# An adaLN block: first modulation as rows, the gate spread by one-hot products, separate banks for each batch's attention

## The chip, the cores and the metric

One core of a Trainium2 chip runs the kernel. The metric is the device time of one execution in microseconds (us), lower is better. TensorE (PE) multiplies, VectorE (DVE), ScalarE (ACT) and GpSimd (POOL) work element by element, SyncE (SP) issues most of the DMAs. TensorE's clock has two levels here, 1.2 and 2.4 GHz; "granted clock" 0.50 and 1.00 in the profile.

## What is computed

```python
mod = (silu(c) @ wmod).reshape(2, 6, 1, 512)         # c: 2 x 512, wmod: 512 x 3072
sa, ca, ga, sb, cb, gb = (mod[:, i] for i in range(6))
ga, gb = (sign(g) * maximum(abs(g), 0.25) for g in (ga, gb))   # sign(0) = 1
h = layernorm(x) * (1 + ca) + sa                     # x: 2 x 512 x 512
x = x + ga * (h @ masked(weight).T + bias)           # 32 x 32 blocks on where the mask has a one
h = layernorm(x) * (1 + cb) + sb
g = silu(lora(h, w1, a1, b1)) * lora(h, w3, a3, b3)  # 512 -> 1376, rank 16, scaling 2
x = x + gb * lora(g, w2, a2, b2)
```

Everything is float32.

## The kernel before

The feature axis of 512 is cut into four slices `k` of 128, the 512 tokens of a batch into four tiles `t` of 128. A product of two float32 matrices is made of three products in the faster fp32r type: high by high, high by low, low by high, where "high" is the rounded value and "low" what is left of it. So each activation and each weight exists as a high part (`ht_hi`, `wa_hi`; written by ACT) and a low part (`ht_lo`, `wa_lo`; written by DVE or POOL). Products on constants at the very start (`WARM_MATMULS`) run while the first loads are under way.

Each engine has one hand-written queue. The order in it is fixed and engines meet at semaphores only, so a waiting instruction holds all that stand behind it.

*Layernorm and turn.* `moment(n)` (DVE), `root` (POOL) and `norm(n)` (DVE or ACT) bring tile n of `work` to mean 0 and variance 1; n runs over 0-3 and 4-7 (attention, batch 0 and 1), 8-11 and 12-15 (feed-forward). `turn(q)` makes four transposes on TensorE, which bring slice k of all four tiles into a PSUM bank with features on partitions. ACT then applies shift and scale twice: `high(q)` writes `ht_hi`, `whole(q)` the unrounded value into `hbuf`, and `low(q)` subtracts them.

*Modulation.* For the attention, shift and scale are made as columns: `mod_column(k)` multiplies 128x128 pieces of `wmod_a` (a copy of a third of `wmod` in another layout, 512 KB each slice) by the two columns of silu(c); one job stands in front of each slice. For the feed-forward they are made as rows, `mod_rows_f`: silu(c), padded to 32 columns, is the stationary operand and four 32-column quads of the array take 256 output columns each; ACT copies the rows out, and two transposes turn them to columns (`columns_f`). `gate_rows(n)` makes the two gates in the same form; ACT and DVE apply sign and maximum.

*Spreading the gate.* The attention's gate must be on all partitions. Four DMAs in ACT's queue (`load_gates`) copy rows of `gates_a` to all 128 partitions of `gate_row_a`, which lies over the mask's tile.

*Attention.* `mask_sum`, `mask_blocks` (one small product) and `mask_weight` make the masked weight of a slice, ACT and DVE split it. `attend(b, k, m)` is the m-th of the three products of slice k, four 512-column matmuls into the four banks `acc`; `attend_last` is slice 3 by tiles. Both batches use the same four banks, so batch 1's bias products (`attend_bias(1)`) wait until DVE has gated batch 0 (`attn_gate`), which waits for the spread gate.

*Feed-forward.* `merge(r)` adds the LoRA product to the r-th weight tile. The loop `for s in range(B * HT)` (22 steps) runs `up` twice (`up_a`, `up_b`) and `down` of the step before. It begins when `turn(8)` to `turn(11)`, `high(8..11)` and `whole(8..11)` are through; their banks are `up_a`, `up_b` and the two `side` banks, and `turn(8)` also waits for DVE to have read `merge(0)` and `merge(1)` from `up_b` and `up_a`.

SP's loads come in this order: x of batch 0, then for each slice `wmod_a`, mask and weight; the attention gate's part of `wmod`; x of batch 1; LoRA pieces 0 and 1; the feed-forward's part of `wmod`; weight tiles.

## Time and profile before

| | |
|---|---|
| median of 3 runs | 280.2 us (279.95 to 282.31) |
| profiled execution, its span | 284.9 us |
| PE / PEld busy | 258.4 / 207.0 us |
| DVE / ACT / POOL busy | 128.4 / 87.6 / 55.6 us |
| DMA | 24.53 MB, mean 86 GB/s |
| mean granted TensorE clock | 0.921 |

The profile is of one execution. Busy time counts what an engine works on and not its waits; PEld is the loading of stationary operands, which overlaps the matmuls. The chain of waits follows the work that ended last back to its releasers. A matmul of two float32 operands stands as two records. Times in the windows and timelines are from the start of the span, and the length of a group of matmuls has the last one's tail in it.

### The profile page before, as it was taken

To read this page: it belongs to the slowest core of one execution; us is meant where nothing else is said; L and a number is where in the kernel's file an instruction comes from. 1 tells how busy PE (TensorE), PEld (TensorE's weight loads), DVE (VectorE), ACT (ScalarE), POOL (GpSimd) and SP (SyncE) were. 2 spreads that over 40 slices of the span, in tenths; PEclk is the share of its full clock that TensorE was granted. 3 is DMA by queue.
4 is the path that set the end of the run, shared out by engine and by line. 5 is a ranking of instruction groups with operands and counts; after the bars stand their busy time and mean duration, and the time that the engine had idled before them with its cause. 6 is when DMAs were issued, how large, how long until landed. Compare 5 with 4: busy or idle time off the path is not lost.

```text
span 284.9 us, 3318 instructions
## 1 busy us (share of the span) xinstructions
PE 258.4 (91%) x1195; PEld 207.0 (73%) x1195; DVE 128.4 (45%) x218; ACT 87.6 (31%) x144; POOL 55.6 (20%) x69
## 2 busy tenths in 40 slices
PE   5799994398875999999999999999999999999991
PEld 3798862385653888888888887788887888888770
DVE  1833251947599399565456554135101111011135
ACT  2341242452933224545654232111011011101110
POOL 1402131655073133033203100005000000000003
PEclk9555799589995999999999999999999999999997
DMA  6999927601512123421332282005800000000004
GB/s 217 371 408 416 363 16 33 30 6 18 185 37 75 37 74 115 131 89 60 90 78 106 56 82 11 2 0 19 156 10 2 0 0 2 0 0 0 2 0 148
DMA packets 12692, 24.53 MB, mean 86 GB/s; under 512 B 1410, under 2 KB 2818, under 8 KB 12676
## 3 DMA queue, kind: packets, MB, share of 16 engines
q1 hardware_dynamic: 11664, 23.65, 28.5%
q10 hardware_dynamic: 1012, 0.67, 4.4%
q8 instruction: 10, 0.16, 0.2%
q14 instruction: 6, 0.05, 0.0%
HBM read 21.16 MB, written 2.10 MB: 82 GB/s over the span
## 4 chain that ended last, share of the span: by engine, by line
PE 82%; DMA 6%; DVE 5%; issue 3%; ACT 3%; SPq 1%; DVEq 0%; ACTq 0%
PE up_a L1003 21%; PE up_b L1003 21%; PE acc L1016 7%; PE acc L1018 7%; PE acc L1017 7%; PE acc L952 6%; PE up_b L885 4%; DMA mask_sb<-gates_a 4%; PE side L867 2%; DMA wmod_a_sb<-in_wmod_a 2%; DVE parts L697 1%; PE side L984 1%; PE acc L937 1%; ACT hbuf L496 1%; DVE wa L707 1%
## 5 line engine op out<-in xcount | busy, mean ns | idle before, releaser
L817 DVE TENSOR_TENSOR g<-up_b,g 128x512 f32<-128x512 f32 (+1 forms) x22 | 15.2, 690 | 73.5 <-PE up_b L1003 73.5
L1016 PE MATMUL acc<-w_hi,g_hi 128*128 128x512 f32 (+1 forms) x88 | 34.9, 396 | 0.0
L1018 PE MATMUL acc<-w_hi,g_lo 128*128 128x512 f32 (+1 forms) x88 | 34.8, 395 | 0.0
L1017 PE MATMUL acc<-w_lo,g_hi 128*128 128x512 f32 (+1 forms) x88 | 34.8, 395 | 0.0
L721 DVE SCALAR_TENSOR_TENSOR raw<-side,raw 128x512 f32<-128x512 f32 (+2 forms) x31 | 20.1, 676 | 27.1 <-PE side L984 20.5
L593 ACT ACTIVATE g<-up_a 128x512 f32<-128x512 f32 (+1 forms) x22 | 13.1, 598 | 61.7 <-PE up_a L1003 61.7
L598 ACT ACTIVATE g_hi<-g 128x512 fp32r<-128x512 f32 (+1 forms) x22 | 13.9, 632 | 52.9 <-DVE g L817 52.9
L390 POOL TENSOR_TENSOR xt<-work,xt 128x512 f32<-128x512 f32 x5 | 6.8, 1377 | 113.0 <-DVE work L736 113.0
L518 ACT ACTIVATE w_hi<-raw 128x512 fp32r<-128x512 f32 (+2 forms) x33 | 20.3, 626 | 26.0 <-DVE raw L721 26.0
L1003 PE MATMUL up_a<-ht_hi,w_hi 128*128 128x512 f32 (+1 forms) x88 | 25.4, 411 | 0.6 <-ACT w_hi L518 0.6
L1003 PE MATMUL up_a<-ht_hi,w_lo 128*128 128x512 f32 (+1 forms) x88 | 24.9, 406 | 0.0
L1003 PE MATMUL up_b<-ht_hi,w_lo 128*128 128x512 f32 (+1 forms) x88 | 24.2, 396 | 0.0
L1003 PE MATMUL up_a<-ht_lo,w_hi 128*128 128x512 f32 (+1 forms) x88 | 24.2, 396 | 0.0
L1003 PE MATMUL up_b<-ht_hi,w_hi 128*128 128x512 f32 (+1 forms) x88 | 24.1, 395 | 0.0
L1003 PE MATMUL up_b<-ht_lo,w_hi 128*128 128x512 f32 (+1 forms) x88 | 24.0, 395 | 0.0
L727 DVE TENSOR_TENSOR w_lo<-raw,w_hi 128x512 fp32r<-128x512 f32 (+2 forms) x33 | 22.4, 707 | 1.9
L1003 PEld LDWEIGHTS up_a<-ht_hi,w_lo 128*128 128x128 f32 (+1 forms) x88 | 16.9, 192 | 4.5
L1003 PEld LDWEIGHTS up_a<-ht_hi,w_hi 128*128 128x128 f32 (+1 forms) x88 | 16.4, 192 | 4.7 <-issue 1.0
L1003 PEld LDWEIGHTS up_a<-ht_lo,w_hi 128*128 128x128 f32 (+1 forms) x88 | 16.6, 188 | 4.3
L1018 PEld LDWEIGHTS acc<-w_hi,g_lo 128*128 128x128 f32 (+1 forms) x88 | 16.6, 188 | 4.1
L1016 PEld LDWEIGHTS acc<-w_hi,g_hi 128*128 128x128 f32 (+1 forms) x88 | 16.5, 188 | 4.0
L1017 PEld LDWEIGHTS acc<-w_lo,g_hi 128*128 128x128 f32 (+1 forms) x88 | 16.5, 188 | 4.0
(107 smaller groups left out, 363.0 us busy)
## 6 DMA issues: line engine op xcount, KB each, us to landing
raw<-in_ffn SPq DMA_DIRECT2D x33, 256.0 KB, 2.7
xt<-in_x SPq DMA_DIRECT2D x8, 256.0 KB, 7.3
wmod_a_sb<-in_wmod_a SPq DMA_DIRECT2D x4, 512.0 KB, 8.0
wmod_sb<-in_wmod SPq DMA_DIRECT2D x2, 1024.0 KB, 13.4
wmod_sb<-in_wmod SPq DMA_DIRECT2D x1, 2048.0 KB, 13.8
out<-xt SPq DMA_DIRECT2D x8, 256.0 KB, 2.9
mask_sb<-in_mask SPq DMA_DIRECT2D x4, 256.0 KB, 8.6
wa<-in_weight SPq DMA_DIRECT2D x4, 256.0 KB, 8.7
```

The lines of the kernel that those rows point to most:

```text
L518: nc.scalar.activation(dst, src, ACT.Copy).then_inc(w_high_ready, 1)
L593: nc.scalar.activation(g[0:w], up_a[0:w], ACT.Silu).then_inc(silu_ready, 1)
L598: nc.scalar.activation(g_hi[s % 2][0:w], g[0:w], ACT.Copy).then_inc(g_high_ready, 1)
L721: nc.vector.scalar_tensor_tensor(w, merge_bank(r)[0:rows, 0:cols], SCALING, w, ALU.mult, ALU.add).then_inc(merged, 1)
L727: nc.vector.tensor_tensor(low_part, src, f32(high), ALU.subtract).then_inc(w_ready, 1)
L817: nc.vector.tensor_tensor(g[0:w], up_b[0:w], g[0:w], ALU.mult).then_inc(g_ready, 1)
L885: last = nc.tensor.matmul(up_b[:, at:at + B], wmod_a_sb[:, k, i, v], silu_c[:, i, 0, 0:B], start=(i == 0), stop=(i == KT - 1))
L952: nc.tensor.matmul(acc[t][:], h[b][:, k, t * P:(t + 1) * P], w[k][:], start=False, stop=False)
L1003: last = nc.tensor.matmul(dst[0:w], w_part[j][:, k, n], h[b][:, k], start=(m == 0 and k == 0), stop=(m == 2 and k == KT - 1))
L1016: nc.tensor.matmul(acc[t][:], hi, down_hi[j][0:w], start=(j == 0), stop=False)
L1017: nc.tensor.matmul(acc[t][:], hi, down_lo[j][0:w], start=False, stop=False)
L1018: last = nc.tensor.matmul(acc[t][:], lo, down_hi[j][0:w], start=False, stop=(j == HT - 1))
```

## The change

- The attention's shift and scale are made as rows, like the feed-forward's: 16 logical products of 256 columns in two halves (`mod_rows_part(0, ...)`), copied by ACT, two transposes, one pair of DVE copies for all slices (`columns`). `wmod_a` and its layout are gone; a third of `wmod` is loaded in two halves of 1 MB instead.
- The gate is made in four quads of 128 columns and spread by four products with a column of the identity, repeated over 128 columns, as stationary operand (`gate_spread`), and ACT copies the bank out (`gate_copy`). The feed-forward's gate is still spread by DMAs, four of 64 KB a batch instead of two of 128.
- Batch 0's attention accumulates in `up_a`, `up_b` and the `side` banks (`front`), batch 1's in `acc`. `turn(0..3)` go to the four `acc` banks, `turn(4..7)` to three of them, `merge(0)` and `merge(1)` to the `side` banks.
- Fifteen products on constants (`fill`) stand at four places of TensorE's queue near the start.
- `attend_last(0)` has only two products a tile, since the first of the three, `attend(0, 3, 0)`, is issued earlier.
- Loads: the two halves of `wmod` are interleaved with the mask and weight of slice 0; x of batch 1 comes ahead of the gate's rows.
- Norms 4 and 5 move from ACT to DVE, `low(0)` from DVE to POOL, and the queues of all engines are reordered.

```diff
-LOW_DVE = (0, 8, 9, 10, 11)
+LOW_DVE = (8, 9, 10, 11)
...
+FILL_MOD, FILL_TURN, FILL_COLS, FILL_H = 6, 2, 4, 3
...
+
+            wmod_sb = sb("wmod_sb", [P, KT, 6 * D], at=early)
...
+        front = [up_a, up_b, *side]
+
         def turn_bank(q):
 
-            return (up_a, up_b)[q % 2] if 2 * KT <= q < 2 * KT + 2 else side[q % 2]
+            i, k = divmod(q, KT)
+            return (acc[k], (acc[1], acc[2], acc[3], acc[1])[k], (up_b, up_a, *side)[k])[i]
+
+        def attn_bank(b, t):
+            return acc[t] if b else front[t]
+
+        def mask_bank(k):
+            return acc[0] if k else side[0]
+
+        def mod_bank(second):
+            return up_a if second else up_b
 
         def merge_bank(r):
-            return (up_b, up_a)[r] if r < FIRST_MERGES else side[SIDE[("merge", r)] % 2]
+            return side[r] if r < FIRST_MERGES else side[SIDE[("merge", r)] % 2]
...
+        def gate_rows_out(n):
+            return (acc[0][:, P:2 * P], front[1][:, 0:P])[n]
...
 
             load_x(0)
-            for k in range(KT):
-                sp.dma_start(wmod_a_sb[:, k], wmod_a[k]).then_inc(wmod_a_loaded[k], 16)
+            load_mod(SHIFT_A, GATE_A, wmod_a_loaded[0], slice(0, KT // 2))
+            sp.dma_start(mask_sb[:, 0], mask[:, 0]).then_inc(mask_loaded[0], 16)
+            load_mod(SHIFT_A, GATE_A, wmod_a_loaded[1], slice(KT // 2, KT))
+            sp.dma_start(wa[:, 0], weight[:, 0]).then_inc(wa_loaded[0], 16)
+            for k in range(1, KT):
                 load_attention(k)
+            load_x(1)
             load_mod(GATE_A, SHIFT_F, wmod_ga_loaded)
-            load_x(1)
             load_lora(0)
             load_lora(1)
             load_mod(SHIFT_F, GATE_F, wmod_f_loaded)
...
+                for q in range(KT):
+                    row = q * QUAD + b
+                    sp.dma_start(gate_row[:, q * P:(q + 1) * P],
+                                 gates_f[row:row + 1].unsqueeze(1).broadcast_to([1, P, P])
+                                 ).then_inc(gate_row_loaded[b], 16)
...
             root(2, 2)
+            low(0)
             low(1)
             low(2)
             low(3)
             root(T, 2)
             root(T + 2, 2)
+            low(KT)
+            low(KT + 1)
+            low(KT + 2)
+            low(KT + 3)
+            spread(0)
             add_x1(0)
             add_x1(1)
-            spread(0)
-            low(KT)
-            low(KT + 1)
             root(2 * T, 2)
             root(2 * T + 2, 2)
-            low(KT + 2)
-            low(KT + 3)
             spread(1)
             for n in range(T, TILES):
...
-            nc.scalar.activation(silu_c[:, :, 1, 0:1], ct[:, :, 1:2], ACT.Silu).then_inc(silu_c_ready, 1)
+            nc.scalar.activation(silu_c[:], ct[:], ACT.Silu).then_inc(silu_c_ready, 1)
...
+                act.wait_ge(centre_ready, n - T * i - 1 + 2 * i)
...
                     act.wait_ge(attn_out, T * (b + 1))
-                else:
-                    act.wait_ge(col_a_ready, k + 1)
+                act.wait_ge(cols_ready, 1 + second)
...
+            def gate_copy(b):
+
+                act.wait_ge(spread_out, b + 1)
+                act.wait_ge(block_on_ready, KT)
+                nc.scalar.activation(gate_row_a[b], acc[2 + b][:], ACT.Copy).then_inc(gate_row_ready, 1)
...
             norm(3)
+            mod_evacuate(0)
             masked_weight_high(0)
             high(0)
             whole(0)
+            masked_weight_high(1)
             high(1)
-            masked_weight_high(1)
             whole(1)
             masked_weight_high(2)
             high(2)
             whole(2)
             masked_weight_high(3)
-            gate_abs(0)
             high(3)
             whole(3)
-            lora_high(0)
-            lora_high(1)
-            act.wait_ge(gates_ready, 1)
-            load_gates(act, 0, 0)
-            load_gates(act, 0, 1)
-            norm(T)
-            norm(T + 1)
             norm(T + 2)
             norm(T + 3)
             high(4)
             whole(4)
+            gate_size(0)
             high(5)
-            mod_evacuate()
             whole(5)
-            lora_high(2)
             high(6)
             whole(6)
-            gate_abs(1)
+            gate_copy(0)
             high(7)
             whole(7)
+            gate_copy(1)
...
             moment(1)
             moment(2)
             moment(3)
-            mask_sum(0)
             norm(0)
             norm(1)
             centres(2)
+            mask_sum(0)
             mask_weight(0)
-            columns_a(0)
+            columns(0)
+            masked_weight_low(0)
             mask_sum(1)
-            masked_weight_low(0)
-            columns_a(1)
             mask_weight(1)
-            low(0)
             mask_sum(2)
             masked_weight_low(1)
-            columns_a(2)
             mask_weight(2)
             mask_sum(3)
             masked_weight_low(2)
-            columns_a(3)
             mask_weight(3)
-            gates_of(0)
-            masked_weight_low(3)
             moment(4)
             moment(5)
+            masked_weight_low(3)
             moment(6)
-            centres(4)
             moment(7)
-            attn_gate(0)
-            attn_gate(1)
-            centres(6)
-            attn_gate(2)
-            attn_gate(3)
+            norm(T)
+            norm(T + 1)
+            centres(T + 2)
+            gates_of(0)
             lora_part(0)
             lora_part(1)
+            for n in range(T):
+                attn_gate(n)
             add_x1(2)
             add_x1(3)
             moment(2 * T)
             moment(2 * T + 1)
-            columns_f()
+            columns(1)
             moment(2 * T + 2)
             moment(2 * T + 3)
+            gates_of(1)
+            lora_part(2)
             for n in range(2 * T, 3 * T):
                 norm(n)
-            gates_of(1)
-            lora_part(2)
             merge(0)
             merge(1)
             weight_low(0)
...
-                pe.wait_ge(normed_by_act, min(2 + T * i, 2 + T))
-                if i != 1:
-                    pe.wait_ge(normed, 2 + T * (i - 1) if i else 2)
-                if q == 2 * KT:
-
-                    pe.wait_ge(merged, FIRST_MERGES)
-                elif q >= 2 and q != 2 * KT + 1:
-
-                    pe.wait_ge(h_ready, q - 1 if q < 2 * KT else q - 3)
+                pe.wait_ge(normed_by_act, min(2 + 2 * i, 4))
+                pe.wait_ge(normed, (2, 4, 8)[i])
+                if i == 1:
+
+                    pe.wait_ge(h_ready, (2, 3, 4, 5)[k])
+                elif i == 2 and k < 2:
+
+                    pe.wait_ge(attn_gated, T)
+                    pe.wait_ge(cols_ready, 2)
+                    pe.wait_ge(gates_ready, 2)
+                elif i == 2:
+
+                    pe.wait_ge(merged, k - 1)
...
-            def mod_column(k):
-
-                pe.wait_ge(wmod_a_loaded[k], 16)
-                if k:
-                    pe.wait_ge(col_a_ready, k)
-                for v in range(2):
-                    at = (2 * k + v) * B
-                    for i in range(KT):
-                        last = nc.tensor.matmul(up_b[:, at:at + B], wmod_a_sb[:, k, i, v], silu_c[:, i, 0, 0:B],
-                                                start=(i == 0), stop=(i == KT - 1))
...
+            def fill(count):
+                for _ in range(count):
+                    nc.tensor.matmul(side[1][:], ht_lo[1][:, 0, 0:P], ht_lo[1][:, 0], start=True, stop=True)
+
+            def mod_rows_part(second, ks):
+
+                for k in ks:
+                    if second:
+                        pe.wait_ge(wmod_f_loaded, 16)
+                        pe.wait_ge(attn_gated, 1)
+                    else:
+                        pe.wait_ge(wmod_a_loaded[k // 2], 16)
+                    for q in range(4):
+                        at = ((SHIFT_A, SCALE_A), (SHIFT_F, SCALE_F))[second][q // 2] * D + q % 2 * HALF
+                        last = nc.tensor.matmul(mod_bank(second)[q * QUAD:(q + 1) * QUAD, 0:HALF], silu_c[:, k],
+                                                wmod_sb[:, k, at:at + HALF], start=(k == 0), stop=(k == KT - 1))
+                if KT - 1 in ks:
+                    last.then_inc(mod_out, 1)
+
+            def columns(second):
+                pe.wait_ge(mod_rows_ready, 1 + second)
+                for c in range(2):
+                    at = second * HALF + c * P
+                    last = nc.tensor.transpose(up_a[:, at:at + P], mod_rows[:, second, c * P:(c + 1) * P], ident[:])
+                last.then_inc(cols_out, 1)
...
                 for k in range(KT):
                     for q in range(4):
-                        at = ((SHIFT_F, SCALE_F)[q // 2] - GATE_A) * D + q % 2 * HALF
...
+                        at = vector * D + q * P
+                        last = nc.tensor.matmul(gate_rows_out(n)[q * QUAD:(q + 1) * QUAD], silu_c[:, k],
+                                                wmod_sb[:, k, at:at + P], start=(k == 0), stop=(k == KT - 1))
                 last.then_inc(gate_out, 1)
+
+            def gate_spread(b):
+
+                pe.wait_ge(gates_ready, 1)
+                pe.wait_ge(h_ready, 6 + b)
+                for q in range(KT):
+                    row = q * QUAD + b
+                    last = nc.tensor.matmul(acc[2 + b][:, q * P:(q + 1) * P], ident[:, row:row + 1].broadcast_to([P, P]),
+                                            gates_a[:], start=True, stop=True)
+                last.then_inc(spread_out, 1)
...
-                nc.tensor.matmul(up_a[:, blocks], const[:, BLOCK_ONES:BLOCK_ONES + P], mask_part[:, blocks],
+                    pe.wait_ge(h_ready, 1)
+                nc.tensor.matmul(mask_bank(k)[:, blocks], const[:, BLOCK_ONES:BLOCK_ONES + P], mask_part[:, blocks],
                                  start=True, stop=True).then_inc(mask_out, 1)
 
             def attend_bias(b):
+                if b:
+
+                    pe.wait_ge(gate_row_ready, B)
+                    pe.wait_ge(h_ready, 2 * KT)
                 for t in range(T):
-                    if b:
-                        pe.wait_ge(attn_gated, t + 1)
-                    nc.tensor.matmul(acc[t][:], ones[:], bias_parts[:], start=True, stop=False)
+                    nc.tensor.matmul(attn_bank(b, t)[:], ones[:], bias_parts[:], start=True, stop=False)
...
-                    nc.tensor.matmul(acc[t][:], ht_hi[b][:, k, tile], wa_hi[k][:], start=False, stop=False)
-                    nc.tensor.matmul(acc[t][:], ht_hi[b][:, k, tile], wa_lo[k][:], start=False, stop=False)
-                    nc.tensor.matmul(acc[t][:], ht_lo[b][:, k, tile], wa_hi[k][:], start=False, stop=True
+                    if b:
+                        nc.tensor.matmul(attn_bank(b, t)[:], ht_hi[b][:, k, tile], wa_hi[k][:], start=False, stop=False)
+                    nc.tensor.matmul(attn_bank(b, t)[:], ht_hi[b][:, k, tile], wa_lo[k][:], start=False, stop=False)
+                    nc.tensor.matmul(attn_bank(b, t)[:], ht_lo[b][:, k, tile], wa_hi[k][:], start=False, stop=True
                                      ).then_inc(attn_out, 1)
...
-                if r == 0:
-
-                    pe.wait_ge(gates_ready, 1)
-                elif r == 1:
-
-                    pe.wait_ge(gates_ready, 2)
+                if r < FIRST_MERGES:
+
+                    pe.wait_ge(attn_gated, T)
...
-            pe.wait_ge(silu_c_ready, 2)
-            mod_column(0)
+            pe.wait_ge(silu_c_ready, 1)
+            mod_rows_part(0, (0, 1))
+            pe.wait_ge(ident_loaded, 16)
+            fill(FILL_MOD)
+            for q in range(KT):
+                turn(q)
             pe.wait_ge(const_loaded, 16)
             mask_blocks(0)
+            fill(FILL_TURN)
+            mod_rows_part(0, (2, 3))
+            fill(FILL_COLS)
+            columns(0)
+            fill(FILL_H)
             pe.wait_ge(ones_ready, 1)
             pe.wait_ge(bias_ready, 1)
+            pe.wait_ge(cols_ready, 1)
+            pe.wait_ge(block_on_ready, 1)
             attend_bias(0)
-            pe.wait_ge(ident_loaded, 16)
-            turn(0)
-            turn(1)
-            mod_column(1)
+            attend(0, 0, 0)
             mask_blocks(1)
-            attend(0, 0, 0)
             attend(0, 0, 1)
-            mod_column(2)
+            attend(0, 0, 2)
             mask_blocks(2)
-            attend(0, 0, 2)
-            turn(2)
             attend(0, 1, 0)
             attend(0, 1, 1)
-            mod_column(3)
             mask_blocks(3)
             attend(0, 1, 2)
-            turn(3)
-            gate_rows(0)
             for m in range(3):
                 attend(0, 2, m)
-            attend_last(0)
-            mod_rows_f()
             turn(4)
             turn(5)
+            gate_rows(0)
+            attend(0, 3, 0)
+            turn(6)
+            gate_spread(0)
+            turn(7)
+            gate_spread(1)
+            attend_last(0)
             attend_bias(1)
             for m in range(3):
                 attend(1, 0, m)
-            columns_f()
-            turn(6)
-            turn(7)
+            mod_rows_part(1, range(KT))
             for m in range(3):
                 attend(1, 1, m)
+            columns(1)
             gate_rows(1)
-            for m in range(3):
-                attend(1, 2, m)
             pe.wait_ge(parts_ready, 2)
             merge(0)
             merge(1)
+            for m in range(3):
+                attend(1, 2, m)
             turn(8)
             turn(9)
...
-        "c": by_feature(c.T),
-        "wmod_a": wmod[:, 0:GATE_A * D].reshape(KT, P, GATE_A, KT, P).transpose(3, 1, 0, 2, 4),
+        "c": np.pad(by_feature(c.T), ((0, 0), (0, 0), (0, QUAD - B))),
```

## Rows read from the trace of the kernel before

**Rows 1.** The page: span, and TensorE's busy time, share and instructions.

```profile
span 284.9 us, 3318 instructions
...
PE 258.4 (91%) x1195; PEld 207.0 (73%) x1195; DVE 128.4 (45%) x218; ACT 87.6 (31%) x144; POOL 55.6 (20%) x69
```

**Rows 2.** The chain of waits in order of time: start us, us, what.

```profile
2.58 5.92 DMA wmod_a_sb<-in_wmod_a
8.63 3.55 PE up_b L885 x16
...
39.84 10.55 DMA mask_sb<-gates_a
...
54.14 1.97 PE side L867 x8
...
89.42 4.68 PE up_a L1003 x12
```

**Rows 3.** Windows: from:to, length, busy of PE, PEld, DVE, ACT, POOL, PEclk, DMA, GB/s.

```profile
7.70:7.90 0.20, 0.00 (x0) 0.00 (x0) 0.20 (x1) 0.20 (x1) 0.00 (x0) 0.50 0.91 307
31.30:31.50 0.20, 0.20 (x2) 0.10 (x2) 0.00 (x0) 0.20 (x1) 0.00 (x0) 0.50 1.08 420
31.70:31.90 0.20, 0.20 (x2) 0.16 (x2) 0.00 (x0) 0.00 (x0) 0.16 (x1) 1.00 1.18 451
54.14:58.80 4.66, 4.66 (x15) 4.08 (x16) 3.64 (x7) 3.47 (x6) 3.91 (x4) 0.50 0.35 25
69.00:72.50 3.50, 2.18 (x16) 1.87 (x15) 2.64 (x5) 1.42 (x3) 2.78 (x3) 1.00 0.56 155
86.20:86.40 0.20, 0.00 (x0) 0.00 (x0) 0.20 (x1) 0.00 (x0) 0.20 (x1) 0.50 0.00 0
93.20:282.00 188.80, 185.41 (x821) 148.72 (x819) 76.57 (x119) 50.86 (x89) 23.93 (x29) 1.00 0.21 45
```

**Rows 4.** Timeline of PE: start us, us, engine, line, operation, count, idle before.

```profile
14.38 1.94 PE L867 MATMUL side<-ident,work 128*128 128x128 f32 x8
...
35.40 0.60 PE L867 MATMUL side<-ident,work 128*128 128x128 f32 x4
35.93 1.93 PE L921 MATMUL up_b<-wmod_sb,silu_c 128*32 128x256 f32 x32
...
38.84 1.08 PE L952 MATMUL acc<-wa_lo,ht_hi 128*128 128x512 f32 x4
...
77.56 1.10 PE L1003 MATMUL up_a<-ht_hi,w_hi 128*128 128x512 f32 x4
```

**Rows 5.** Timeline of ACT, same columns.

```profile
12.76 1.52 ACT L467 ACTIVATE work<-xt,centre,rstd 128x512 f32<-128x512 f32 x2 [4.55 <-DVE centre L636]
...
35.51 0.63 ACT L534 ACTIVATE wa_hi<-wa 128x512 fp32r<-128x512 f32 x1 [3.91 <-DVE wa L677]
...
72.31 0.78 ACT L487 ACTIVATE ht_hi<-up_a,shift,one_plus 128x512 fp32r<-128x512 f32 x1
```

**Rows 6.** Timeline of DVE.

```profile
39.75 0.69 DVE L618 BATCH_NORM_STATS2 stats<-xt 128x6 f32<-128x512 f32 x1
40.47 0.18 DVE L620 BATCH_NORM_AGGREGATE moments<-stats 128x2 f32<-128x6 f32 x1
...
53.66 1.27 DVE L697 SCALAR_TENSOR_TENSOR parts<-parts,const,lora_raw 128x256 fp32r<-128x256 f32 x2
...
68.16 1.28 DVE L697 SCALAR_TENSOR_TENSOR parts<-parts,const,lora_raw 128x1024 fp32r<-128x1024 f32 x1
```

**Rows 7.** Timeline of POOL.

```profile
39.94 1.28 POOL L367 TENSOR_TENSOR ht_lo<-hbuf,ht_hi 128x512 fp32r<-128x512 f32 x1 [6.91 <-ACT hbuf L496]
...
41.99 0.71 POOL L354 TENSOR_TENSOR rstd<-rstd,exponent 128x2 f32<-128x2 f32 x1
```

**Rows 8.** Issues of x1 on SP's timeline, then their median landing in us.

```profile
9.29 5.70 SPq L295 DMA_DIRECT2D xt<-in_x  x4
...
xt<-in_x SPq DMA_DIRECT2D x4, 256.0 KB, 9.8
```

113 lines of the change are left out of this document (40 added, 73 removed).

## The prediction

> **What bounds the kernel now.** I read the page first. Its span is 284.9 us and the matmul engine is busy for 91% of it [rows 1], but that average hides two parts. In the windows, the stretch from 93.2 to 282 us has TensorE busy for 185.4 of 188.8 us at full clock [rows 3]: the feed-forward loop, which the diff leaves alone and which can only start earlier or later. Everything the change can win or lose lies ahead of it. I then read the chain of waits in order of time [rows 2]. It shows two costs: the front waits for the first 512 KB of `wmod_a` (5.92 us) and then runs 16 two-column products in 3.55 us; and from 39.84 us a DMA that spreads the gate takes 10.55 us, over which TensorE stands still until `turn(4)` at 54.14. The granted clock [rows 3] adds a third. It is 0.50 (1.2 GHz) from 7.7 us, after an idle spell, is still 0.50 at 31.3, full (2.4 GHz) at 31.7, and 0.50 again from 54.14 to 58.8, after the gate's stall. Last I read each engine's timeline for the prices [rows 4 to 7].
>
> **Prices.** Eight transposes, which is two `turn`s, are 1.94 us at 1.2 GHz, and four are 0.60 at 2.4 GHz, both with their tail (a `turn` is about 0.9 and 0.45 back to back) [rows 4]. Four 512-column products are 1.08 with their tail, 0.93 apart when full, 0.23 each, so about 0.45 each at half. `gate_rows`, 16 logical products on 32-column quads of 256 columns, is 1.93 at full; a modulation of the same form costs the same, 0.96 for half of it, and twice that at half clock. ACT: a modulation pass 0.78, a weight copy 0.63, two norms 1.52 [rows 5]. DVE: a moment 0.69 and 0.18, about 0.8 the pair; other 512-column passes (norm, merge, masked weight, gating) I put at 0.6 to 0.7 from that 0.69; two early LoRA parts 1.27, the third 1.28 [rows 6]. POOL: a low part 1.28, a root 0.71 [rows 7] behind a short add, 1.15 the pair by estimate.
>
> **The walk through the front, after the change.** I go through the queues in their new order; times are us from the start of the span.
>
> 1. *First modulation.* The first half of the rows is 1 MB instead of 512 KB. The first piece lands at 2.58 + 5.92 = 8.5; 524 KB more at the 420 GB/s of [rows 3] is 1.3, so 9.85. TensorE has stood idle since its warm-up and is at 0.50. Half the rows: 1.9, to 11.8. Six constant products: 2.7, to 14.5. They cost nothing: `turn` needs ACT's norms, which end at 12.76 + 1.52 = 14.3 [rows 5], as now, since the root and centres ahead of them are unmoved (`mask_sum(0)` only moves behind them).
> 2. *Four turns together.* TensorE has then been busy without a break since 9.85. I take two at half (1.8) and two at full (0.9): 17.2. Mask product 0.2 (an estimate: one product, so not above a 512-column one), two fills 0.5, the second half rows 1.0: 18.8. ACT's copy (0.4) lies under four fills (0.9): 19.7; two transposes 0.25, DVE's two small copies 0.3: 20.3. Three fills and the four bias products run to 21.6, over `high(0)` (to 21.1). The first product starts at 21.6, where it starts at about 20 now: the front alone is 1.6 later.
> 3. *Three slices of batch 0.* Nothing but one mask product (0.2) now stands between the products, where each slice had a column job of 3.5 at half clock. A slice is 2.8 + 0.2, against ACT's 0.63 + 0.78 + 0.78. DVE's chain mask product, compare, masked weight, then ACT's copy and `high`, is queued one slice ahead and costs some 0.1 a slice. The third slice ends at 31.0.
> 4. *New gap.* `turn(4)` is late next. ACT's `whole(3)` ends near 30.2; POOL's `low(3)` stands ahead of the roots in its queue (1.3: 31.5), two roots 2.3, DVE's centres 0.3, ACT's two norms 1.5 and some tenths between engines: 36.05. TensorE waits 5 us. At 86.2 us TensorE stands in a shorter wait and has lost the clock [rows 3], so I charge a restart at half. `turn(4)` is still 18.1 earlier than the 54.14 of now, since the gate's DMA is gone, but `attend(0,3)` now lies behind it.
> 5. *Gate by products.* `turn(4)`, `turn(5)` 1.8, `gate_rows` of 128 columns at half clock 1.9: 39.8. From there ACT sets the pace: size 0.3, six passes of `high` and `whole` 4.7, two copies of the spread gate 1.2 (a 512-column copy, priced as the weight copy): 46.1. `gate_spread` has no row: at least 0.25 for four 128-column products, at most a `turn`'s 0.9 each at half clock; I take 0.5, hidden under ACT either way but for 0.4. TensorE's own work here (`attend(0,3,0)`, two turns, `attend_last`) fits beneath: about 9.5 at worst, the clock returning on the way.
> 6. *Batch 1.* It has its own banks, so its bias products wait for the two gate copies alone: 46.2. The gating of batch 0 starts at about 48, after both LoRA parts, which wait in DVE's queue for ACT's copies behind `gate_copy(1)`; `mod_rows_part(1)` needs one gated tile at about 50 and finds it. TensorE: bias 0.9, slice 2.8, rows 1.9, slice 2.8, columns 0.25: 54.9. Then DVE carries it: columns 0.3, two moments 1.6, gates 0.6 (two 128-column passes, an estimate at half of a 512-column one each), third LoRA part 1.3, four norms 2.4: 61.1. TensorE's gate rows, two merges and a slice (4.3) lie beneath that. The two merges on DVE (1.3), two weight copies on ACT with the first overlapping (0.7): `high(8)` at 63.2.
>
> `high(8)` is at 72.31 now [rows 5] and the first `up` product follows at 77.56 [rows 4]; that stretch keeps its instructions and queues. The second step starts with the row at 89.42 [rows 2], after a DVE queue of LoRA parts and merges whose loads were issued once the third LoRA part was done: that moves from about 69.4 to 58.7, so it shifts too. The sum: 72.3 - 63.2 = 9.1 us less.
>
> Priced at nothing: the removed memset of `silu_c` (POOL idles until the moments), the padded `c` (16 times 4 KB, tiny beside the loads), eight small feed-forward gate DMAs in place of four (SP issues them while the loop runs, and the second batch's are needed at its end; uncovered, some us at the very end), and the swap of `x1` with the attention gate's rows: now `x1` is issued last of the two, from 9.29 to 14.99, and takes 9.8 more [rows 8], so both lie there by 24.8, before the moments of batch 1 want them near 27. The page gives the span as the profiled execution's own time; against its 284.9 the sum is 275.8. The median of the runs shown is 280.2, 4.7 below that span; I subtract the same 9.1: **271.1 us**.
>
> **A rule that speaks against step 2.** In [rows 3] the stretch from 69.0 to 72.5 has 2.18 us of TensorE work, more than half of it `turn`s, and the clock stays full; the stretch to 31.7, in which it came back, was mostly 512-column products with one `turn`. Neither shows whether turns bring it back. The Trainium skill, "TensorE: Matmul & The Clock Gate", Part 4 on PE-mode transpose, says that the full clock doesn't engage for transposes since they don't count as busy in the same way. By it steps 2 and 5 would both restart late, near 280 as worked out under the rivals, where my sum stands at 271.
>
> **Rivals.**
> - *A late clock at the front only.* The fills are too short and the clock returns only among the slices. Two more turns at half 0.9, fills, rows and columns 2.0, bias and part of the first slice 2: 4.9 later, 276.0. For it: TensorE was busy without a break from 8.6 to 31 and stayed at 0.50. Against: the largest part of that was two-column products, and none of those are left.
> - *Late at both places.* Turns and 128-column products do nothing for the clock. In step 5 then `attend_last`, the bias and part of a slice run at half too, 4 to 4.5 more: about 280, no change. For it: nothing in the rows shows the clock returning over turns alone. Against: it stayed full over two of them and a wait [rows 3]. The rule of the Trainium skill quoted above would end here.
> - *Slower: half clock all the way to `turn(8)`.* The 19 us of full-rate work behind step 5 and the slices ahead take twice as long, some 15 and 9 more, of which the gap of step 4 absorbs 5: about 290. It decides from the point where products worth 9 us at full clock run at half. Against: in both places now, 4 to 5 us of 512-column products brought the clock back.
> - *Shorter gap in step 4.* The engines are quicker by 2 to 3 us, or the clock is kept: 268.
>
> **How the numbers follow.** Forecast 0.55; late at the front 0.2; late at both 0.08; half all the way 0.04; shorter gap 0.1; 0.03 for what I don't see. The likeliest case's own range is 269 to 273.5 (the split of the clock in step 2, +-0.9; the spread's bounds, 0.4; tenths between engines in six steps, up to 1.5). With the late front and the shorter gap, 267 to 277 leaves out less than 2 in 10. A measurement of this kernel can tell about 1% from no change, that is below 277.4 or above 283.0: faster 0.87, same 0.08, slower 0.05.
>
> **What would show it.** After the change: first products of the slices near 21.6 with the clock full by then (a granted 0.5 there is the late front); a TensorE gap of 5 us ahead of `turn(4)` near 36, put down to ACT's norm; `attend_bias(1)` near 46 released by ACT's gate copy; `turn(8)` near 61 released by DVE's norm; first `up` near 68.5; and from there the same intervals as before. I am wrong if the loop's own part changes length, or if a wait stands where I name none.

## The result

The kernel after the change takes 278.74 us (median of 20 runs, 277.36 to 280.78), the kernel before 282.27 us in the 20 runs beside it (278.9 to 287.98). The ratio is 0.9946, 95% interval 0.9921 to 0.9971: 1.5 us faster against a forecast of 9.1. The ratio leaves out executions more than 1.5% above the kernel's fastest, which are seven of the 20 runs of before (five of them near 287 us) and none of after. Over all 20 of each the means are 282.6 and 278.9 us, 3.7 apart; experiments 2 and 4 show why before has the long ones and that they belong to what the change removes.

The profile of after, its span and TensorE's busy time:

```profile
span 277.0 us, 3318 instructions
...
PE 250.8 (91%) x1196; PEld 197.7 (71%) x1196; DVE 128.4 (46%) x212; ACT 87.0 (31%) x144; POOL 57.2 (21%) x69
```

The two profiles differ by 284.9 - 277.0 = 7.9 us where the ratio gives 1.5. That is the question of this study. The lines of after that answer to [rows 2] and [rows 4], from TensorE's timeline:

```profile
11.09 1.93 PE L890 MATMUL up_b<-wmod_sb,silu_c 128*32 128x256 f32 x16 [5.02 <-DMA wmod_sb<-in_wmod]
12.95 2.93 PE L878 MATMUL side<-ht_lo 128*128 128x512 f32 x6
15.68 2.68 PE L866 MATMUL acc<-ident,work 128*128 128x128 f32 x16
...
22.94 0.39 PE L960 MATMUL up_a<-wa_hi,ht_hi 128*128 128x512 f32 x1
...
32.35 0.63 PE L960 MATMUL side<-wa_hi,ht_lo 128*128 128x512 f32 x2
37.91 1.97 PE L866 MATMUL acc<-ident,work 128*128 128x128 f32 x8 [4.93 <-ACT work L476]
39.81 1.70 PE L916 MATMUL acc<-wmod_sb,silu_c 128*32 128x128 f32 x32
...
47.80 1.09 PE L945 MATMUL acc<-bias_parts,ones 128*128 128x512 f32 x4
...
62.35 0.63 PE L866 MATMUL up_b<-ident,work 128*128 128x128 f32 x4 [1.09 <-issue]
...
69.25 1.14 PE L1009 MATMUL up_a<-ht_hi,w_hi 128*128 128x512 f32 x4
```

The first slice's products start at 22.94, the third slice ends at 33.0, `turn(4)` comes after a wait of 4.93 us that ACT's norm ends, the bias products of batch 1 stand at 47.80, `turn(8)` at 62.35, the first `up` at 69.25. The walk had 21.6, 31.0, 36.05 after 5 us, 46.2, 61.1 and 68.5. The kernel was later than that by up to 2.0 us and by 0.75 at the walk's end; the loop behind is 277.0 - 69.25 = 207.8 us, and 284.9 - 77.56 = 207.3 before [rows 1, 4]. So the times of the new kernel's model held within 2 us (what ended its fifth step did not, see below). What did not hold is what it was subtracted from.

### The profile page after: what moved, and what is told of

It is laid out like the page before. It is cut to its first block, busy times and chain, and to the rows that moved or that the text cites. A ratio compares the mean times of both kernels' runs of the same rounds, so it can differ in the third digit from the quotient of the medians.

```text
span 277.0 us, 3318 instructions
## 1 busy us (share of the span) xinstructions
PE 250.8 (91%) x1196; PEld 197.7 (71%) x1196; DVE 128.4 (46%) x212; ACT 87.0 (31%) x144; POOL 57.2 (21%) x69
## 4 chain that ended last, share of the span: by engine, by line
PE 79%; DVE 8%; issue 4%; ACT 3%; DMA 3%; POOL 1%; SPq 1%; DVEq 0%; ACTq 0%; POOLq 0%
PE up_a L1009 22%; PE up_b L1009 21%; PE acc L1022 7%; PE acc L1024 7%; PE acc L1023 7%; DMA wmod_sb<-in_wmod 3%; PE acc L960 2%; PE side L878 2%; PE acc L866 2%; DVE parts L697 2%; PE side L990 2%; DVE stats L626 1%; ACT hbuf L502 1%; PE up_b L890 1%; ACT ht_hi L493 1%
## 5 line engine op out<-in xcount | busy, mean ns | idle before, releaser
L721 DVE SCALAR_TENSOR_TENSOR raw<-side,raw 128x512 f32<-128x512 f32 (+2 forms) x33 | 21.4, 677 | 27.4 <-PE side L990 20.8
L1009 PEld LDWEIGHTS up_a<-ht_hi,w_lo 128*128 128x128 f32 (+1 forms) x88 | 16.9, 192 | 4.5
L1022 PEld LDWEIGHTS acc<-w_hi,g_hi 128*128 128x128 f32 (+1 forms) x88 | 16.5, 188 | 4.0
L1023 PEld LDWEIGHTS acc<-w_lo,g_hi 128*128 128x128 f32 (+1 forms) x88 | 16.5, 188 | 3.9
## 6 DMA issues: line engine op xcount, KB each, us to landing
wmod_sb<-in_wmod SPq DMA_DIRECT2D x1, 2048.0 KB, 15.6
```

The lines of the kernel that those rows point to most:

```text
L721: nc.vector.scalar_tensor_tensor(w, merge_bank(r)[0:rows, 0:cols], SCALING, w, ALU.mult, ALU.add).then_inc(merged, 1)
L1009: last = nc.tensor.matmul(dst[0:w], w_part[j][:, k, n], h[b][:, k], start=(m == 0 and k == 0), stop=(m == 2 and k == KT - 1))
L1022: nc.tensor.matmul(acc[t][:], hi, down_hi[j][0:w], start=(j == 0), stop=False)
L1023: nc.tensor.matmul(acc[t][:], hi, down_lo[j][0:w], start=False, stop=False)
```

## Experiments

Each kernel ran beside the kernel before on the same chip.

**1. The kernel before, again** (`before_again`, unchanged).

> The kernel before, unchanged, in new executions. Theory A (the clock): the profiled execution of before, 284.9 us of span, was a long one, because its granted clock came back only at 31.5 us, behind three column jobs at half clock (3.2 us each where the fourth took 1.68). Then a profile with a span near 278 shows a column job of 1.7 us earlier than 31 us and the first up product 4 to 6 us earlier than 77.56, and the runs' mean clocks go with their spans. Theory B (the loads): the long execution had slow DMAs (the gate's 10.55 us or the first load's 5.92 us); then a short one has those shorter and the column jobs unchanged. Theory C: all executions have the front of the first profile and differ in the loop.

Median 287.08 us (282.07 to 287.37, 6 runs), with before's 11 runs beside it at 286.81 (279.63 to 287.5); the profiled execution has a span of 285.6. TensorE's timeline, the four column jobs and the first `up`:

```profile
9.26 3.54 PE L885 MATMUL up_b<-silu_c,wmod_a_sb 128*128 128x2 f32 x16 [3.60 <-DMA wmod_a_sb<-in_wmod_a]
...
16.65 3.41 PE L885 MATMUL up_b<-silu_c,wmod_a_sb 128*128 128x2 f32 x16
...
23.91 3.41 PE L885 MATMUL up_b<-silu_c,wmod_a_sb 128*128 128x2 f32 x16
...
33.11 1.84 PE L885 MATMUL up_b<-silu_c,wmod_a_sb 128*128 128x2 f32 x16
...
78.28 1.12 PE L1003 MATMUL up_a<-ht_hi,w_hi 128*128 128x512 f32 x4
```

It is the first profile once more: two column jobs behind the first at half clock, the fourth at full; the clock is back at 32.4 us. On this chip such executions are the rule. The expected short one was not caught here. That the runs' mean clocks go with their times came out in part: 0.921 or 0.922 in 23 of the 24 runs near 287 us whose clock is on record (0.963 in the other), but 0.950 or 0.968 near 282.8 and 0.958 to 0.974 near 279.7.

**2. The kernel before, a third look** (`before_look2`, unchanged).

> The kernel before once more, to catch an execution other than the long one (spans of 284.9 and 285.6, both with the clock back at 31.5). Times of before come in three groups, near 279.6, 282.8 and 287.2 us. Theory A, sharpened: the groups are three moments at which the clock comes back in the front, so a profile of the middle group has it back near 23 to 28 us with the fourth and third column job at 1.8 us, and one of the short group has it back before 21 us. Rival: the front is the same and the loop or a DMA differs.

One run: 280.15 us, span 278.4. The same lines and, from the windows, the granted clock (the column before the last two):

```profile
9.15 3.31 PE L885 MATMUL up_b<-silu_c,wmod_a_sb 128*128 128x2 f32 x16 [3.08 <-DMA wmod_a_sb<-in_wmod_a]
...
16.50 1.84 PE L885 MATMUL up_b<-silu_c,wmod_a_sb 128*128 128x2 f32 x16
...
20.37 1.84 PE L885 MATMUL up_b<-silu_c,wmod_a_sb 128*128 128x2 f32 x16
...
25.60 1.84 PE L885 MATMUL up_b<-silu_c,wmod_a_sb 128*128 128x2 f32 x16
...
47.34 1.97 PE L867 MATMUL side<-ident,work 128*128 128x128 f32 x8 [7.91 <-ACT work L467]
...
70.00 1.10 PE L1003 MATMUL up_a<-ht_hi,w_hi 128*128 128x512 f32 x4
```

ACT's timeline has the pass `high(8)`:

```profile
64.75 0.78 ACT L487 ACTIVATE ht_hi<-up_a,shift,one_plus 128x512 fp32r<-128x512 f32 x1
```

The windows:

```profile
9.40:16.00 6.60, 6.40 (x26) 5.52 (x27) 5.25 (x14) 2.04 (x3) 3.15 (x5) 0.50 1.02 372
16.50:43.00 26.50, 22.39 (x176) 17.49 (x174) 11.12 (x29) 10.26 (x16) 5.87 (x7) 1.00 0.97 301
```

For comparison, `turn(4)` in the first profile of before:

```profile
54.14 1.97 PE L867 MATMUL side<-ident,work 128*128 128x128 f32 x8 [7.88 <-ACT work L467]
```

Same program, and the first job is at half clock here too (3.31), but the clock is back by 16.5 us instead of 31.7 [rows 3]. The column jobs take 1.84 each and the first `up` starts at 70.00, 7.6 us ahead of the 77.56 of [rows 4]. The gate's stall is as long as in the first profile (TensorE waits 7.91, and 7.88 there). Against this execution the 69.25 of after is 0.75 us earlier, and the whole 1.4 (278.4 - 277.0), close to the ratio's 1.5. The other 0.65 lies in the loop, where the clock falls in the first step of both and is back at 85.5 us in after, at 87.9 here. All 65 runs of before beside these kernels fall into three groups: 18 from 278.9 to 280.8 us, 18 from 282.1 to 283.5, 29 from 286.5 to 288.5, with medians of 279.7, 282.8 and 287.2. Spans of before lie some 1.8 us below times (those of after 1.6), so the first profile (284.9) is of the last group. The ratios of the experiments are taken against the lower two groups together, whose shares differ from set to set (their means are 280.6 to 282.1 us), so small differences are read from medians too.

**3. More products at the very start** (`before_warm`).

```diff
-WARM_MATMULS = 10
+WARM_MATMULS = 20
```

> Before with 20 constant products at the start in place of 10, so that TensorE is busy from 1.4 us to about when the first modulation weights land (8.6 us). Theory A: the clock is full when the column jobs begin in every execution, each is 1.7 us instead of 3.3, the long executions are gone and the median is 276 to 279, no slower than after the change (277 to 279). Theory B or C: the median stays within 0.3% of before, with the same spread of 279 to 288.

284.75 us (282.41 to 288.06), ratio 1.0037 (0.9948 to 1.0125): no gain, and theory A's forecast missed. The median lies between two groups of three runs, near 282.6 and near 287; none is near 279.7. The profile, an execution of the long group, shows the first job at full clock and the second at half:

```profile
9.25 1.92 PE L885 MATMUL up_b<-silu_c,wmod_a_sb 128*128 128x2 f32 x16 [0.96 <-DMA wmod_a_sb<-in_wmod_a]
...
15.04 1.94 PE L867 MATMUL side<-ident,work 128*128 128x128 f32 x8 [1.66 <-issue]
16.77 3.41 PE L885 MATMUL up_b<-silu_c,wmod_a_sb 128*128 128x2 f32 x16
```

```profile
11.00:12.60 1.60, 1.19 (x7) 0.98 (x7) 1.54 (x3) 0.00 (x0) 1.30 (x3) 1.00 0.93 283
12.80:15.00 2.20, 0.57 (x2) 0.00 (x0) 1.67 (x6) 1.58 (x3) 0.31 (x1) 0.50 1.04 411
```

The windows put the loss at 12.7 us, among the four bias products: ahead of the wait of 1.66, and behind waits of 0.96 and 0.32 us and the two-column job. A clock that is full when the work starts is not kept through it; whether the waits or the two-column products cost it, this run does not tell.

**4. Products in those holes too** (`before_fill`: 20 at the start and these).

```diff
             attend_bias(0)
+            for _ in range(8):
+                nc.tensor.matmul(side[1][:], ht_lo[1][:, 0, 0:P], ht_lo[1][:, 0], start=True, stop=True)
             pe.wait_ge(ident_loaded, 16)
```

> Before with 20 products at the start and 8 constant products more between the bias products and turn(0), where TensorE waited 1.66 us with 20 products alone and then lost the clock. Theory A: the clock is kept or comes back before the second column job in most executions, the column jobs take 1.8 us each instead of 3.4, the group near 287 is gone and the median is 276 to 279. Rival: two-column products lower the clock whatever stands around them; then the times stay in the three groups, median above 281.

280.25 us (278.71 to 281.52, 12 runs), ratio 0.9928 (0.9892 to 0.9965), beside 17 runs of before with a median of 286.54. The upper two groups are gone with 18 constant products and nothing else; the median is 1.3 us above the top of what I expected. All four column jobs take 1.84 or 1.85 us, but the clock still dips:

```profile
12.00:16.80 4.80, 4.71 (x35) 4.04 (x33) 2.36 (x7) 3.60 (x5) 0.13 (x1) 1.00 1.02 404
17.00:20.20 3.20, 3.20 (x9) 2.53 (x9) 2.73 (x7) 2.08 (x3) 0.74 (x1) 0.50 1.05 408
```

TensorE is busy for 4.71 of the 4.80 us before the fall, with constant products to 14.0, two turns and the second column job. So a hole is not needed for the clock to fall, and the rival of two-column products is not excluded. Theory A stands for what the groups are: the profiles of this program show the early and the late return, and the middle one was seen in the same front of experiment 5. This kernel, whose DMAs and stalls are those of before, is 0.7 to 1.5 us slower than after by the medians (278.74 and 279.55) and no slower by the ratio (0.9928 against 0.9946): 18 constant products in the old kernel bring most of what the whole change brings.

**5. The gate's spread left out of before** (`before_nogate`).

```diff
-            load_gates(act, 0, 0)
-            load_gates(act, 0, 1)
...
-                nc.vector.tensor_tensor(mid[n % T], acc[t][:], gate_row_a[b], ALU.mult).then_inc(attn_gated, 1)
+                nc.vector.tensor_tensor(mid[n % T], acc[t][:], xt[:, b, t], ALU.mult).then_inc(attn_gated, 1)
```

> Before with the four DMAs that spread the attention's gate left out; the gating multiplies by x instead, which lies there already, so the gate is left out of the result. It prices the stall by itself: 54.14 us for turn(4) should become about 46.5 (ACT's norms right behind their moments, nothing in ACT's queue ahead), so 6 to 8 us less than before, if the stall is what the profile says. If the stall is hidden in ordinary executions, less than 2 us.

272.91 us (270.92 to 280.21, 4 runs), ratio 0.9669 (0.9553 to 0.9785), some 9 us. The four runs look like the three groups again (270.9 and 271.1; 274.7; 280.2); if they are, they lie 8.7, 8.1 and 7.0 us under those of before, so the stall is worth 7 to 9 us, about what I expected. It shrinks to 1.66 us, and the clock is kept through it.

```profile
28.72 1.84 PE L881 MATMUL up_b<-silu_c,wmod_a_sb 128*128 128x2 f32 x16
...
44.20 1.09 PE L863 MATMUL side<-ident,work 128*128 128x128 f32 x8 [1.66 <-ACT work L467]
```

In this execution the clock came back at 23.4 us, between the other two, with the third and fourth job at 1.84: the middle group. So there was a stall worth 7 to 9 us to remove, and the change removed it. It must have put something in its place.

What made the stall is also a matter of order. DVE's timeline in experiment 2:

```profile
43.68 1.29 DVE L707 TENSOR_TENSOR wa<-acc,mask_sb 128x512 f32<-128x512 f32 x2 [6.71 <-DMA mask_sb<-gates_a]
```

The centres for ACT's last two norms stand behind these two gatings in DVE's queue and wait with them for the gate's DMA. Putting them ahead, or issuing the four DMAs from another queue than ACT's, are cheaper changes that were not tried.

**6. The spread left out of after** (`after_nogate2`: no `gate_spread`, no `gate_copy`, gating by x).

> After the change with the spreading of the attention's gate left out (no spread products, no ACT copies, the gating multiplies by x, so the gate is left out of the result). Theory: the spread has been moved from DMA to TensorE and ACT and still costs 2 to 3 us there, two copies of 0.6 in ACT's queue and the waits between spread and turn; so 2 to 3 us less than after the change, against 8 us for the same cut in before. If it is hidden now: under 0.5 us.

276.81 us (276.49 to 277.32), ratio to before 0.9818 (0.9731 to 0.9904), so 1.9 to 2.7 us below after (278.74 and 279.55), about as expected. The spread still costs that much; the rest of the 7 to 9 went elsewhere. With the spread left out of both kernels, these runs lie 5.8 us above the lowest two of before (270.9 and 271.1): without the stall the new order is the slower one.

**7. The spread by DMA again, banks kept** (`after_dmagate`).

```diff
+            for b in range(B):
+                for q in range(KT):
+                    row = q * QUAD + b
+                    act.dma_start(gate_row_a[b][:, q * P:(q + 1) * P],
+                                  gates_a[row:row + 1].unsqueeze(1).broadcast_to([1, P, P])
+                                  ).then_inc(gate_row_a_loaded[b], 16)
```

> After the change with the one part undone: the attention's gate is spread by DMAs again (eight of 64 KB, issued by ACT behind whole(7)) in place of the one-hot products and copies; the banks of their own stay. If the one-hot spread is what takes the stall away: gating of batch 0 starts at 54 to 57 us instead of 49.2, 4 to 7 us slower than after the change. If the separate banks alone take it away: within 1 us of after the change.

290.52 us (289.25 to 291.19), ratio 1.0344 (1.0268 to 1.0419): 11 to 12 us slower than after, more than expected. ACT's and TensorE's timelines:

```profile
44.62 12.21 ACTq L580 DMA_DIRECT2D mask_sb<-gates_a  x8
57.20 1.99 ACT L543 ACTIVATE parts<-lora_raw 128x256 fp32r<-128x256 f32 x3 [11.86 <-issue]
```

```profile
60.03 3.64 PE L897 MATMUL up_a<-wmod_sb,silu_c 128*32 128x256 f32 x32 [10.58 <-DVE wa L714]
```

Eight issues hold ACT's queue for 12.21 us, the LoRA parts wait behind them, the gating behind those, and TensorE stands for 10.58 us. With the DMAs in this place the separate banks alone don't take the stall away, because `mod_rows_part(1)` needs a gated bank; the one-hot products do. DMAs from SP's queue, which would not hold ACT, were not tried with the new banks either.

**8. Without the fills** (`after_nofill`: all four counts 0).

> After the change without its 15 constant products. Theory A (the clock of the front decides): the clock comes back later, the four turns run at half to their end (3.6 us instead of 2.5) and the first slices too, 2 to 5 us slower than after the change. If the fills do nothing for the clock: within 0.5 us, or up to 1 us faster, since they delay the columns.

279.96 us (278.29 to 280.68), ratio 0.9934 (0.9871 to 0.9997). After is 278.74 and 279.55 in its two sets of runs, so the fills are worth 0.4 to 1.2 us with ranges that overlap, less than I expected of a late clock. The profile has the four turns at half clock throughout:

```profile
15.27 3.65 PE L866 MATMUL acc<-ident,work 128*128 128x128 f32 x16 [2.59 <-ACT work L476]
```

They take 3.65 instead of 2.68, the clock is back by 19.5, before the slices, and skipping the fills gives back part of the loss. In five profiles of after and its variants with the fills (experiments 6 and 9 to 12) it is back between 15.7 and 16.5 us. So none of these profiles has it late, and half of the rows costs only 0.9 us more at half clock (1.93 against 1.07); that this is why after has no groups is likely and was not tested by itself.

**9. After, again** (`after_again`).

> The kernel after the change once more, beside the versions below. Theory A: its times do not fall into groups as those of before do (279.6, 282.8, 287.2), because no two-column products are left in the front; median 278 to 279.5, all within 1%, on a chip where most executions of before are near 287.

279.55 us (278.11 to 280.46, 10 runs), ratio 0.9946 (0.9901 to 0.9991), beside 17 runs of before with a median of 286.79. One group of 2.4 us against three that spread over 9 us, as expected. After varies with the clock too, but less: this profile (span 278.2) has a stretch at half clock from 70.5 to 74 us, at the loop's start, that the first profile of after (277.0) does not have.

**10. Fills in the gap ahead of `turn(4)`** (`after_gapfill`).

```diff
+            pe.wait_ge(h_ready, KT)
+            for _ in range(18):
+                nc.tensor.matmul(acc[3][:], ht_lo[1][:, 0, 0:P], ht_lo[1][:, 0], start=True, stop=True)
             turn(4)
```

> After the change with 18 constant products in the 4.9 us gap ahead of turn(4), so that the clock is full when it ends. The clock's price in the second gap: turn(4), turn(5) 1.0 us instead of 1.9 and the gate rows 1.1 instead of 1.7, so attend_bias(1) 1.5 us earlier and the whole 1 to 2 us less than after the change. If ACT sets the pace of that stretch from turn(4) on alone: under 0.5 us.

276.33 us (275.9 to 277.43), ratio 0.9808 (0.975 to 0.9865): 2.4 to 3.2 us below after's two sets, more than the 1 to 2 expected.

```profile
31.92 4.28 PE L1062 MATMUL acc<-ht_lo 128*128 128x512 f32 x18
...
37.04 1.09 PE L866 MATMUL acc<-ident,work 128*128 128x128 f32 x8 [0.84 <-ACT work L476]
38.06 1.08 PE L916 MATMUL acc<-wmod_sb,silu_c 128*32 128x128 f32 x32
```

The two turns take 1.09 instead of 1.97 and the gate rows 1.08 instead of 1.70 (1.94 in experiment 9). From `turn(4)` to batch 1's bias products it is 8.4 us, where after has 9.9 and the profile of experiment 9 has 10.9.

**11. Fills in the loop's first wait too** (`after_tuned1`).

```diff
+                if s == 0:
+                    pe.wait_ge(attn_gated, 2 * T)
+                    for _ in range(16):
+                        nc.tensor.matmul(acc[0][:], ht_lo[1][:, 0, 0:P], ht_hi[1][:, 0], start=True, stop=True)
```

> after_gapfill (18 constant products ahead of turn(4), 276.3 us) with 16 more in the 4.2 us wait of the loop's first step, where the clock is lost too and the next twelve products take 5.0 us instead of 2.8. If the clock is kept: 1.5 to 2.2 us less than after_gapfill, about 274.5. If the wait is too long for them or they delay the merge: within 0.5 us.

274.44 us (273.85 to 274.81), ratio 0.9776 (0.9719 to 0.9834): 1.9 less again, as expected. Its timeline, then that of after at the same place:

```profile
74.51 3.81 PE L1114 MATMUL acc<-ht_hi,ht_lo 128*128 128x512 f32 x16
78.76 1.17 PE L1009 MATMUL up_a<-ht_hi,w_hi 128*128 128x512 f32 x4 [0.21 <-ACT w_hi L524]
```

```profile
79.74 0.79 PE L994 MATMUL side<-parts 128*128 128x512 f32 x1 [4.21 <-DVE raw L721]
81.10 2.05 PE L1009 MATMUL up_a<-ht_hi,w_hi 128*128 128x512 f32 x4 [0.56 <-ACT w_hi L524]
```

The four products behind the wait take 1.17 instead of 2.05.

**12. A shorter norm chain** (`after_tuned2`: `moment(4)` behind `mask_sum(1)`, roots 4 and 5 ahead of `low(3)`).

> after_tuned1 with the queues ahead of turn(4) reordered: moment(4) behind mask_sum(1), where VectorE waits 1.3 us, and root(4,5) ahead of low(3). The norm chain is what ends the gap: it loses one moment (0.8) and part of a low (0.5), so turn(4) comes 0.7 to 1.3 us earlier and the whole is 0.5 to 1.3 us less than after_tuned1. If the last moment's load (x1) were the limit: no change.

274.04 us (272.98 to 274.62), ratio 0.9756 (0.9703 to 0.981). Only 0.4 less, at the edge of what the runs tell. `turn(4)` comes 0.2 us earlier (36.87 against 37.04). The moved instructions and their neighbours became slower; POOL's and DVE's timelines:

```profile
30.91 0.66 POOL L360 TENSOR_SCALAR rstd<-moments 128x2 f32<-128x2 f32 x1
```

```profile
33.03 1.39 DVE L637 TENSOR_SCALAR work<-xt,moments,rstd 128x512 f32<-128x512 f32 x2
35.09 0.16 DVE L644 SCALAR_TENSOR_TENSOR centre<-moments,rstd 128x2 f32<-128x2 f32 x1 [0.67 <-POOL rstd L363]
```

The short add of the first root takes 0.66 where it took 0.22, the two norms take 1.39 next to POOL's `low(3)` where they took 1.00, and the centres wait for POOL as before. What slows them was not tested. It is the fastest version of the study, 2.4% below the kernel before.

## Why the prediction was wrong

**The subtraction.** The failing step is the last sentence of the sum, "4.7 below that span; I subtract the same 9.1". The 9.1 was made against an execution whose `high(8)` stood at 72.31 [rows 5]. In experiment 2 it stands at 64.75, 7.6 us earlier: the clock came back 15 us sooner, which spares two column jobs and some slices at half clock ahead of `turn(4)` (6.8 us) and brings the clock back sooner behind the gate's stall (0.8). Only executions of the long group pay these 7.6. The three runs shown (279.95, 280.2 and 282.31) were of the other two groups. I saw that the profile's span was 4.7 us above the median and took it for an offset; as a time (1.8 us above the span) that execution was 6.5 us longer, and what made it longer is mostly work that the change removes. Experiments 1, 2 and 4 show it. Against the 64.75 the same 63.2 leaves 1.6 us instead of 9.1, and the ratio gives 1.5. That the two agree so well is in part luck, since the front of after came 0.8 later than forecast and the loop's clock gave 0.65 back. Had I put 1.6 us on the sum's own end, 275.8, the forecast would have been 277.4, within 0.5% of the 278.74.

**Step 1** was early by 1.2 us: the first half of the weights for the rows landed at 10.95 and its products started at 11.09, not 9.85. The chain of waits of after says

```profile
2.58 8.37 DMA wmod_sb<-in_wmod
```

I had priced its second 512 KB at the full rate behind the first piece of `wmod_a` (5.92 [rows 2]). In these 8.37 us the DMAs moved 2.7 MB (326 GB/s), of which x of batch 0 and this half are 2.0, so the pieces issued behind it took a share.

**Step 2** was right: six fills at half clock, the clock back within the turns (16 in 2.68), first product at 22.94 with step 1's delay in it. The late clock of the rivals did not come, and the transposes did not hold it off. Without the fills (experiment 8) the clock came back by 19.5 us with nothing ahead of it since 12.7 but a wait, 16 transposes (15.27 to 18.9), a mask product and the start of the rows. The rule quoted from the Trainium skill, that transposes don't engage the full clock, did not hold in this kernel. Of the rows weighed on it, 69.0 to 72.5, one reading was off: turns are 0.9 of the 2.18 us there, not more than half.

**Steps 3 and 4** were right: three slices in 10.0 us (9.4 forecast), a new gap of 4.93 us ended by ACT's norm and a restart at half clock (1.97 for two turns). The gap stood in the working at its full price; together with what moved behind it, it uses up what the removed stall gives. In the execution of experiment 2 the third slice ends at 34.0 and `turn(4)` is at 47.34; after has 33.0 and 37.91, 9.4 us earlier. But `turn(4)` to the first `up` is 31.3 us in after and 22.7 in that execution: slice 3 (3.0), the gate rows (1.6) and the feed-forward's rows (1.9), which lay ahead of the gate's stall, now stand behind `turn(4)`, and so do the new spread products (1.9). Ahead of that the sides are nearly even: the first product starts 4.5 us later than the 18.43 of experiment 2, and the three slices take 10.0 us instead of 15.6, since no column jobs, turns and gate rows stand between them. The change takes out a wait of 7.9 and puts in one of 4.9. (The prediction let TensorE stand still over the DMA's 10.55 us; it worked until 46.3 and waited 7.88.) The working had all of these terms; only against the long execution did they leave 9.

**Step 5** was right in its length (9.9 us against 10.1), but not in what sets it. It had ACT's gate copies release batch 1's bias products. TensorE's timeline and ACT's:

```profile
43.49 1.13 PE L926 MATMUL acc<-gates_a,ident 128*128 128x128 f32 x8 [0.42 <-ACT hbuf L502]
44.46 0.60 PE L866 MATMUL acc<-ident,work 128*128 128x128 f32 x4
44.97 1.13 PE L926 MATMUL acc<-gates_a,ident 128*128 128x128 f32 x8
45.85 0.48 PE L973 MATMUL up_a<-wa_lo,ht_hi 128*128 128x512 f32 x1
```

```profile
46.69 0.59 ACT L537 ACTIVATE mask_sb<-acc 128x512 f32<-128x512 f32 x1
```

The second copy ends at 47.28 and the bias products follow `attend_last` at 47.80 without a wait: TensorE itself is the last to finish. A spread takes 0.97 and 0.88 us at full clock to the start of what follows, each more than the 0.5 taken and about the 0.9 called the most at half clock; its products stand as two records each, those of a turn as one. That the length came out is luck in part. Without the spread (experiment 6) the bias products do wait for ACT, 1.06 us.

**Step 6** was right in mechanism, as far as times show it (DVE's norms end at 62.25 and `turn(8)` starts at 62.35, though the view puts the wait to "issue"), and within 0.4 us in length (14.6 against 14.9).

## What to carry to other kernels

When a profile's span stands above the runs' times, find out which part of it is long before a difference is priced against it: a stretch that ran at half clock in one execution may run at full in the next, and a change that removes such work looks larger than it is. Price the new kernel to its end and compare that end with the runs, beside the difference. Count what moves behind a removed stall: a stall worth 7 to 9 us was there and was removed, and 1.5 us came out, because a new wait came in and work that had stood ahead of the stall was laid behind it. And try the cheap remedy first: 18 constant products in the old kernel came within 1.5 us of the whole change.

## What the runs showed of the hardware

With the same front, TensorE's clock comes back at 16.2, at 23.4 or at 31.6 to 32.4 us, after the same work from 9 us on; the times of the kernel before lie at 279.7, 282.8 or 287.2 us. What chooses among the three was not found: the first job started at 9.15 in the early case, at 8.63 and 9.26 in the late ones. A clock that had been full was lost at 12.7 us behind a two-column job and waits of 0.96 and 0.32 us (experiment 3), and at 16.9 with waits of no more than 0.1 us but a two-column job again (experiment 4); with 18 constant products in the front none of 12 runs was in the upper two groups. In the profile's first microseconds the clock column can't be relied on: it reads 1.00 in after from 0 to 37 us, where six 512-column products at 12.95 took 2.93 us, which is half clock; their pace tells it.
